# Attention and quantized product in one kernel: another order ahead of the first unit, and other steps for the side work

## The reference

```python
q = rope(rmsnorm(xn @ Wq + bq, qn_w))                       # 16 heads of 128
w = softmax over each 4 rows of (xn @ Wcmp + bcmp)
entries = weighted sums of 4 rows of xn                     # 256 per batch
ck = rope(rmsnorm(entries @ Wk + bk, kn_w)); cv = entries @ Wv + bv
ctx_sparse = softmax over the top 8 causal scores q.ck, times cv
lk, lv = rope(rmsnorm(xn @ Wlk + blk, kn_w)), xn @ Wlv + blv
ctx_local = softmax(q.lk in a band of 128) times lv
attention = ((ctx_sparse + ctx_local) * 0.5) @ Wo + bo
ffn = fp8(xn * scale) / scale  @  fp8(W2 * scale1) / scale1
out = x + attention + ffn
```

## Time and profile before

| | us |
|---|---|
| median of 3 runs | 2624.01 |
| range of the runs | 2623.75 to 2624.39 |
| profiled execution, its own time | 2621.21 |
| its span in the profile | 2619.4 |
| TensorE busy | 2528.2 (97%) |
| VectorE busy | 2001.0 (76%) |

### The profile page before, as it was taken

One profiled execution on the slowest core, in us unless ns is written; L12 is line 12 of the kernel. 1 busy time (PEld: TensorE's weight loads), 2 busy tenths in 40 slices (PEclk: granted clock), 3 DMA queues, 4 the chain that ended last, 5 costly groups with the idle time before them and its releaser, 6 DMA issues.

```text
span 2619.4 us, 55065 instructions
## 1 busy us (share of the span) xinstructions
PE 2528.2 (97%) x15288; PEld 2227.1 (85%) x15320; DVE 2001.0 (76%) x6447; ACT 1641.4 (63%) x4641; POOL 1561.2 (60%) x2757
## 2 busy tenths in 40 slices
PE   4799999999999999999999999999999999999998
PEld 3677888888888888888888888888888888888887
DVE  5688887888878887777877877778777776677775
ACT  2556666666666666666666666666666666666665
POOL 3576776777677555555556655555555655555554
PEclk9899999999999999999999999999999999999999
DMA  3313321333333212222234221212233221222101
GB/s 106 131 62 99 117 93 50 101 113 102 126 121 110 85 52 75 90 67 72 77 105 138 86 83 60 86 52 75 86 109 121 93 70 32 67 69 69 57 14 49
DMA packets 168290, 220.73 MB, mean 84 GB/s; under 512 B 17842, under 2 KB 89012, under 8 KB 167988
## 3 DMA queue, kind: packets, MB, share of 16 engines
q1 hardware_dynamic: 167988, 217.23, 25.0%
HBM read 156.35 MB, written 60.82 MB: 83 GB/s over the span
## 4 chain that ended last, share of the span: by engine, by line
PE 74%; ACT 0%; issue 0%; DVE 0%; ACTq 0%
PE bQK L514 7%; PE bQK L515 7%; PE bQK L516 7%; PE bVC L588 6%; PE bP L570 6%; PE bVC L585 5%; PE bY L600 4%; PE bVC L530 4%; PE bVC L531 4%; PE bVC L532 4%; PE bY L601 4%; PE bY L602 4%; PE bT L540 3%; PE bS L562 3%; PE bS L561 3%; PE bS L560 3%
## 5 line engine op out<-in xcount | busy, mean ns | idle before, releaser
L1265 POOL TENSOR_TENSOR t<-raw,tB 128x128 f32<-128x128 f32 x512 | 227.2, 465 | 624.2 <-DVE raw L883 624.1
L761 ACT ACTIVATE ch<-bVC,blT 128x128 fp32r<-128x128 f32 x512 | 159.9, 363 | 505.8 <-PE bVC L588 504.9
L514 PE MATMUL bQK<-wh,xh 128*128 128x512 f32 x1024 | 428.5, 418 | 1.1 <-DVE raw L883 1.1
L1219 POOL TENSOR_TENSOR r<-ss,mh 128x4 f32<-128x4 f32 x256 | 289.2, 1130 | 226.8 <-DVE ss L900 226.6
L515 PE MATMUL bQK<-wl,xh 128*128 128x512 f32 x1024 | 405.4, 396 | 0.0
L516 PE MATMUL bQK<-wh,xl 128*128 128x512 f32 x1024 | 403.7, 394 | 0.0
L928 DVE CUSTOM_DVE_ANT_0 P<-bS,cst 128x256 f32<-128x256 f32 (+1 forms) x512 | 203.7, 398 | 157.4 <-PE bS L562 156.5
L530 PE MATMUL bVC<-wh,xh 128*128 128x256 f32 x1024 | 311.3, 304 | 0.6 <-DVE cl L977 0.6
L722 ACT ACTIVATE raw<-raw,r 128x128 f32<-128x128 f32 x512 | 177.9, 395 | 188.7 <-POOL r L1219 185.5
L728 ACT ACTIVATE P<-P,nm,r 128x256 f32<-128x256 f32 (+1 forms) x512 | 295.3, 583 | 0.0
L532 PE MATMUL bVC<-wh,xl 128*128 128x256 f32 x1024 | 289.8, 283 | 0.0
(11 more groups left out here) (144 smaller groups left out, 6944.1 us busy)
## 6 DMA issues: line engine op xcount, KB each, us to landing
wh<-kept SPq DMA_DIRECT2D x144, 256.0 KB, 4.1
wl<-kept SPq DMA_DIRECT2D x144, 256.0 KB, 4.6
kept<-wh SPq DMA_DIRECT2D x48, 256.0 KB, 3.1
kept<-wl SPq DMA_DIRECT2D x48, 256.0 KB, 3.4
woh<-kepto SPq DMA_DIRECT2D x48, 256.0 KB, 3.4
wol<-kepto SPq DMA_DIRECT2D x48, 256.0 KB, 3.8
out<-acc SPq DMA_DIRECT2D x32, 256.0 KB, 2.1
ini<-in_hidden_states SPq DMA_DIRECT2D x24, 256.0 KB, 4.1
```

The lines of the kernel that those rows point to most:

```text
L514: e.matmul(bQK[:, :], a, b, start=kt == 0, stop=False)
L1219: e.tensor_tensor(r4[:, u % 4], ss[:, u % 4], mh[:, 0:4], ALU.pow).then_inc(S["r4"], 1)
```

## The change

Eight things are moved. Most lie ahead of unit 0 or in the first ten steps; the new `tile_base` and `ffn_base` reach through the whole program.

1. The constants (five DMAs on d_c) are issued by ScalarE, which then runs one `Exp` on a constant. SyncE's list begins with tile 0, chunk 0, tile 1, chunk 1, tiles 2 to 4.
2. Ahead of unit 0 TensorE and VectorE have loops of their own, with the order of calls shown in the diff.
3. In those steps `logits` goes to the second bank of bS and no longer to bY (`FIRST_TILES` = 5).
4. `tables` moves from VectorE (step -5) to GpSimd (step -2).
5. One chunk of weights is split per step ahead of unit 0, not two.
6. The first block of keys is one step sooner (`BLOCK_LAGS` 4 and 5, not 5 and 6); `turn_ck` and `hi_ck` stand ahead of `turn_x` and `hi_x` in a step; `entries` of tiles 4 to 7 is one step later.
7. W2 is some steps later: loads at steps 2 to 5, casts at 4 to 7, `excess` and `rejoin` at 5 to 8, `quant_nan` at 6 to 9.
8. Tiles 8 and up start 4 steps later; the quantized product of tiles 0 to 7 is 3 steps later, of the others 5. `new_ck` of a batch's second block is 3 steps later.

```diff
 def tile_base(t):
-    return t - AHEAD if t < 8 else 64 * (t // 8 - 1) + 5 + 7 * (t % 8)
+    return t - AHEAD if t < 8 else 64 * (t // 8 - 1) + 9 + 7 * (t % 8)
-BLOCK_LAGS = {"kv": (5, 7), "put": (5, 7), "rope": (5, 7), "turn": (6, 9), "hi": (6, 9), "lo": (6, 9)}
+BLOCK_LAGS = {"kv": (4, 5, 7), "put": (4, 5, 7), "rope": (4, 5, 7), "turn": (5, 6, 9), "hi": (5, 6, 9), "lo": (5, 6, 9)}
 def ffn_base(t):
-    return 7 + 7 * t if t < 8 else tile_base(t) + 4
+    return 10 + 7 * t if t < 8 else tile_base(t) + 5
-    out = [("w", 0, c, c // 2 - AHEAD) for c in range(6)]
+    out = [("w", 0, c, c - AHEAD) for c in range(6)]
+        def logits_of(t):
+            return (bY if t >= FIRST_TILES else bS[1])[:, 0:128]
...
# TensorE
+            for s in range(FIRST, 0):
+                if tile_at(s, "turn") is not None:
+                    turn_x(tile_at(s, "turn"))
+                    logits(tile_at(s, "turn"))
+                if tile_at(s, "et") is not None:
+                    entries(tile_at(s, "et"))
...
# ScalarE
+            e.dma_start(cst[:, :], consts).then_inc(S["d_c"], 16)
+            e.dma_start(wcb[:, :], Wcmp.rearrange("n a -> a n").broadcast_to([128, 512])).then_inc(S["d_c"], 16)
+            e.dma_start(bcm[:, :], bc(bcmp, 1)).then_inc(S["d_c"], 16)
+            e.dma_start(isc[:, 0:1], bc(sc0, 1)).then_inc(S["d_c"], 16)
+            e.dma_start(isc[:, 1:2], bc(sc1, 1)).then_inc(S["d_c"], 16)
+            e.wait_ge(S["ones"], 1)
+            e.activation(junk[:, 0:1], mh[:, 0:1], ACT.Exp)
-                if 1 <= s <= KT:
-                    cast_w2(s - 1)
+                if 4 <= s < 4 + KT:
+                    cast_w2(s - 4)
...
# VectorE
+            for s in range(FIRST, 0):
+                norm_stats(tile_at(s, "stats"))
+                if s == FIRST:
+                    e.wait_ge(S["d_c"], 16 * 5)
...
+                if tile_at(s, "wm") is not None:
+                    weights4(tile_at(s, "wm"))
+                if tile_at(s, "norm") is not None:
+                    normalise(tile_at(s, "norm"))
+                if tile_at(s, "max") is not None:
+                    group_max(tile_at(s, "max"))
+                    lo_x(tile_at(s, "lo"))
...
-                if 2 <= s < 2 + KT:
-                    excess(s - 2)
-                    rejoin(s - 2)
-                if s == 2 - AHEAD:
-                    tables()
+                if 5 <= s < 5 + KT:
+                    excess(s - 5)
+                    rejoin(s - 5)
...
# GpSimd
+                if s == -2:
+                    tables()
```

More of the change, by code:

```diff
@@ L88, in block_at @@
     for k in range(NTT // 4):
-        if tile_base(4 * k + 3) + BLOCK_LAGS[stage][k >= 2] == s:
+        if tile_base(4 * k + 3) + BLOCK_LAGS[stage][min(k, 2)] == s:
             return k
@@ L617, in logits, with entries @@
                 e.wait_ge(S["dg"], t + 1)
+                if t >= FIRST_TILES:
+                    e.wait_ge(S[free["Y"][0]], free["Y"][1])
+                    free["Y"] = ("eg", t + 1)
+                elif t:
+                    e.wait_ge(S["eg"], t)
+                e.matmul(logits_of(t), onef[:, :], dg[:, :], start=True, stop=True).then_inc(S["bc"], 1)
+            def entries(t):
+                e.wait_ge(S["wm"], t + 1)
                 if free["Y"]:
                     e.wait_ge(S[free["Y"][0]], free["Y"][1])
[L620 to L625, removed]
                 for kt in range(KT):
@@ L657, in run_tensor @@
             e.wait_ge(S["d_c"], 16 * 5)
-            for s in range(FIRST, LAST):
+            for s in range(FIRST, 0):
[4 more added lines that the diff above has]
+                    entries(tile_at(s, "et"))
+            for s in range(LAST):
                 u0, u1, u2, u3, u4, u5 = (unit_at(s, lag) for lag in range(6))
@@ L661, in run_tensor @@
                     proj_qk(u0, 0)
+                if block_at(s, "turn") is not None:
+                    turn_ck(block_at(s, "turn"))
                 if tile_at(s, "turn") is not None:
                     turn_x(tile_at(s, "turn"))
-                if block_at(s, "turn") is not None:
-                    turn_ck(block_at(s, "turn"))
                 if u2 is not None:
@@ L837, in run_scalar @@
                     exp_w(tile_at(s, "ew"))
+                if block_at(s, "hi") is not None:
+                    hi_ck(block_at(s, "hi"))
                 if tile_at(s, "hi") is not None:
@@ L1115, in lo_ck @@
                 e.tensor_tensor(lo, src, f32(hi), ALU.subtract).then_inc(S["lo_ck"], 1)
[L1117 to L1130, removed]
-                e.tensor_tensor(cA[:, :, :], cA[:, :, :], w[:, 0:64].unsqueeze(1).broadcast_to([128, 2, 64]), ALU.mult)
-                for k in range(2):
-                    d_, s_ = slice(32 * k, 32 * k + 32), slice(32 - 32 * k, 64 - 32 * k)
-                    e.tensor_tensor(cB[:, :, d_], cB[:, :, d_], w[:, s_].unsqueeze(1).broadcast_to([128, 2, 32]),
-                                    ALU.mult)
-                e.tensor_tensor(wqk[:, :], wrow[:, 64:128], wrow[:, 192:256], ALU.mult).then_inc(S["tab"], 1)
@@ L1144, in run_vector @@
+            for s in range(LAST):
                 u0, u1, u2, u3, u4, u5 = (unit_at(s, lag) for lag in range(6))
                 if block_at(s, "lo") is not None:
-                    if tile_at(s, "lo") is not None:
-                        lo_x(tile_at(s, "lo"))
                     lo_ck(block_at(s, "lo"))
@@ L1155, in run_vector @@
                     neg_max(u2)
-                if tile_at(s, "lo") is not None and block_at(s, "lo") is None:
+                if tile_at(s, "lo") is not None:
                     lo_x(tile_at(s, "lo"))
@@ L1321, in run_gpsimd @@
                     rope_rest(u0)
-                if u2 is not None and u2 % 64 == 63 and u2 + 1 < NU:
-                    new_ck(u2 // 64 + 1, 1)
+                if u2 is not None and u2 >= 64 and u2 % 64 == 2:
+                    new_ck(u2 // 64, 1)
                 if ffn_at(s, 2) is not None:
                     quant_nan(KT + ffn_pos(ffn_at(s, 2)))
-                if 3 <= s < 3 + KT:
-                    quant_nan(s - 3)
+                if 6 <= s < 6 + KT:
+                    quant_nan(s - 6)
                 if block_at(s, "rope") is not None:
```

63 lines of the change are left out of this document (38 added, 25 removed).

## The result

The changed kernel takes 2592.01 us (median of 4 runs, 2590.12 to 2592.75); the kernel before, timed beside it, 2623.88 (2622.0 to 2624.39). The ratio is 0.9879, 95% interval 0.9862 to 0.9896. That is 31.9 us less; forecast were 27. The two profiled executions are 29.8 us apart (2621.21 and 2591.37).

The account below looks back on a forecast made before the run. TensorE, busy 97% of the span, was taken to bound the kernel, with gains mostly ahead of unit 8. A lead of 20.6 plus 6.6 us gave 27.2 off 2621.21, 2594.0, plus 2.8: 2597 us, range 2584 to 2611.

Parts of the forecast that it names:

- the lead at unit 8: How much sooner unit 8's bias addition starts than in the kernel before (165.6): 20.6 us.
- First transpose: Ahead of unit 0: constants land at 7.0, so the first transpose starts at 9.2 (8.0 to 11.2), 3.0 us sooner.
- The ring: Steps ahead of unit 0: VectorE alone sets the pace, a tile every 5.2 us instead of 7.05, bounds 4.5 and 7.05.
- The tables: Ahead of unit 0, on GpSimd: 7.0 us, bounds 6.2 and 14, from about 27 to 34, costing nothing on the path.
- Units 0 to 2: Projection to unit 0 11.3 us, then 17.7 to unit 1 and 11.0 to unit 2; lead 18.6 there.
- Units 2 to 8: One wait of 2.2 us goes, W2 stages change steps: 2 us off 73.4, bounds 6 off and 5 on.
- The meetings: Keys' product and quantized product in one step, in six blocks from the third on: 1.1 us each, 6.6 saved apart.
- The thick step in the first batch: Normalisation, an `excess` and an `init` fall into one step: 0 us taken, bounds 8 off and 10 on.
- Rival 5: First batch: `normalise`, `excess` and `init` in one step delay TensorE in each of 8 rounds, 22 us lost; chance 0.04.
- rival 2: First batch gets smoother too, 10 us of waits for low halves go as well: 2587; chance 0.17.
- Rivals 1, 3, 4: Lead given back in units 0 to 8, 0.21; ring stays at 7.05, 0.08; DMAs limit ahead of unit 0, 0.10.

Follow-up runs that it names:

- keys late: The changed kernel with the first block of keys one step later (lags 5 and 6 as before), all else kept: 2589.5 us, ratio 0.9873.
- W2 early: The changed kernel with the four W2 stages alone back in their old steps 1 to 6: 2592.2 us, ratio 0.9882.

## Why the prediction was right

*Total.* 27 us forecast, 31.9 measured, 29.9 by the last units. The range, 2584 to 2611, held it. That the total came so near is in part luck: the lead at unit 8 was 8.1 us more than the 20.6 forecast, and behind it came 1.2 instead of 6.6.

*First transpose.* Forecast 9.2 with bounds 8.0 to 11.2, measured 11.33, outside by 0.1. The failing term is the landing of the constants: I took 7.0, it was 9.29. I had let the sooner issue count and not the 0.5 MB more in front. The runs fit that: with 0.5 MB less, and no chunk issued until they were there, the constants landed at 8.09; back on SyncE, with the last issue 1.4 us later and 0.5 MB less in front, at 8.78. The former run also has the five in another order, so how much each of these weighs is open. The Trainium skill (DMA: Bandwidth & Descriptors, "Issuing engines are not separate DMA queues") had said that only issuing time is saved; here not even that shows, with 9.29 against 8.98. What made the first transpose 0.85 us sooner all the same is the statistic that now lies ahead of the wait.

*The ring.* Forecast 5.2 a tile, measured 5.14 to 5.30. Two runs show what it needs: without the free bank 6.1 to 9.5, with VectorE's old order 10.1 to 11.1. GpSimd's splits cost 0.9 to 1.0 and not 0.7, 0.36 in the product and 0.62 in `dg` in the step shown; VectorE's own work was 4.3 and not 4.5, and the two errors cancel.

*The tables.* 7.0 forecast, 7.7 measured, hidden as said but for 0.3. Their load on VectorE in step -1 came to 1.4 us, where the prediction had a possible 2 for steps -1 and 0. "The tables' place is the largest piece" is right for the step: 8.4 us for step and engine together, of which only 1.4 for the engine.

*Units 0 to 2.* 11.3, 17.7 and 11.0 forecast; the parts measured are 9.8 (35.77 to 45.57), 16.9 and 11.2. The chain of step 1 ran as written, through GpSimd's powers and ScalarE's scaling. The reason I gave for the keys, that they cost at first and win later, fell with the run of keys late: they win back their cost and no more.

*Units 2 to 8.* The term that was mis-sized. I took 2 us off for the moved W2 stages and the entries, bounds 6 off and 5 on; it was 10.1 (73.4 to 63.3), and in the ten other kernels with W2 late 8.1 to 10.2. I had weighed VectorE's work over the whole stretch and found it the same. But ahead of unit 4 VectorE was what TensorE waited for, and behind it there was room: 21.3 us against 15.7 in units 2 to 4. W2's move gives 7.3 of it at unit 8, of which 3.6 stay by the profiles (the medians show 0.2, inside the intervals). Together with tile 8's move and the rest of item 8 it is 10 us at the end, shown on both kernels; how these 10 divide is only partly known.

*The meetings.* 6.6 forecast, 3.4 measured by the medians of the run that restores them, 2.5 for the five behind unit 64. Two things were wrong in the term. The row that it rests on lacks a matmul in each group, so 1.1 is 0.9. And I counted what the old place costs and put the new place at nothing, where `ini` is waited for.

*The thick step in the first batch.* I took 0. The waits for parked low halves went from 10.0 to 5.2 us, that for the low half of the context grew from 0.6 to 3.4, and units 8 to 64 with the work that has moved behind unit 64 came to 0.9 us more than before (576.6 + 3.5 against 579.2), W2's work among it. With W2 early they take 573.0 + 3.5, 2.7 less than before. Rival 5 did not show; of rival 2's 10 us no more than these 3.

*Rivals 1, 3, 4.* The clock rose sooner, not later: granted 0.80 from unit 1 to 2 against 0.66. The ring opened. The loads did hold the first transpose by 2 us, not the tiles behind it.

## What to carry to other kernels

Work off the critical engine isn't the same wherever it stands: ask in which steps the helping engine is the one waited for, and weigh its load there, not over a long stretch. An order on one engine can need its partner's: free bank, VectorE's order and TensorE's order together made 5.2 us a tile, without the bank it was 6.1 to 9.5, without VectorE's order 10.1 to 11.1. Ahead of a first wait on a DMA count the bytes in front, and not only the time of issue. Read the count of a matmul group before taking the idle time before it for a wait, and when a stage moves away from a wait, ask what it will wait for in its new place.

## What was not expected of the hardware

The same five small and medium loads landed at 9.29 issued by ScalarE from 0.73 to 3.14, and at 8.98 issued by SyncE until 4.52, with 0.5 MB more in flight beside them in the first case. A VectorE operation of 128 columns (`dg`) took 0.91 us beside a GpSimd subtraction of 512 columns, and 0.29 where none ran beside it.
